# Scores of 8-wide heads in two row tiles of TensorE, and the additive mask as a 128-row matmul, in a two-layer decoder

## Time and profile before

| | |
|---|---|
| median of the runs | 787.25 us (786.77 to 790.87) |
| span of the profiled execution | 788.8 us; a time of its own beside the span is not listed |
| instructions | 12952 |
| TensorE matmul (PE) | 633.0 us busy, 80% |
| TensorE weight load (PEld) | 513.6 us, 65% |
| VectorE (DVE) | 505.0 us, 64% |
| ScalarE (ACT) | 381.3 us, 48% |
| GpSimd (POOL) | 230.7 us, 29% |
| mean granted clock of TensorE | 0.869 of 2.4 GHz |

### The profile page before, as it was taken

The page is one execution under the profiler, slowest core; times in us unless marked ns, Lnnn a source line. Parts: engine busy times, 40 slices in busy tenths (PEclk is TensorE's granted clock), DMA queues, the critical chain, the costliest instruction groups (busy, mean ns, idle before and its releaser), DMA issues. The chain is left out here.

```text
span 788.8 us, 12952 instructions
## 1 busy us (share of the span) xinstructions
PE 633.0 (80%) x3779; PEld 513.6 (65%) x3786; DVE 505.0 (64%) x1221; ACT 381.3 (48%) x966; POOL 230.7 (29%) x254
## 2 busy tenths in 40 slices
PE   4898885999999968699889999979999988781006
PEld 3777774777777756467668888868777776430006
DVE  3788983656675745744544444447677676469886
ACT  3778883445444532133235444435455463484615
POOL 3555552323222211356500000014334331005220
PEclk9899996989997958899979999989899797695558
DMA  5400000001000000000000000001010000000001
GB/s 158 160 11 10 10 13 14 21 21 28 24 20 17 0 1 1 0 1 2 1 11 7 11 10 7 17 14 27 20 26 21 19 17 0 1 0 0 0 0 54
DMA packets 30649, 15.29 MB, mean 19 GB/s; under 512 B 18513, under 2 KB 29841, under 8 KB 30610
## 3 DMA queue, kind: packets, MB, share of 16 engines
q1 hardware_dynamic: 30610, 14.82, 6.7%
HBM read 10.09 MB, written 1.05 MB: 14 GB/s over the span
## 5 line engine op out<-in xcount | busy, mean ns | idle before, releaser
L330 PE MATMUL bank<-a_mov,a_stat 128*128 128x256 f32 x256 | 84.2, 459 | 12.0 <-issue 10.2
L514 DVE TENSOR_REDUCE rowmax<-bank 128x8 f32<-128x512 f32 x64 | 44.2, 691 | 62.2 <-PE bank L330 61.4
L330 PEld LDWEIGHTS bank<-a_mov,a_stat 128*128 128x128 f32 x256 | 50.6, 219 | 28.7 <-issue 23.0
L1213 POOL TENSOR_TENSOR e_hid<-e_gated,e_relu 128x512 f32<-128x512 f32 x32 | 40.6, 1270 | 57.0 <-DVE e_gated L1328 56.8
L1088 PEld LDWEIGHTS bank<-body_sb,e_hid 128*128 128x128 f32 x288 | 37.7, 196 | 22.0 <-issue 13.9
L139 POOL TENSOR_TENSOR xb<-X,made_bias 128x128 f32<-128x128 f32 x32 | 14.6, 457 | 117.2 <-DVE r L149 103.8
L1190 ACT ACTIVATE e_relu<-bank 128x512 f32<-128x512 f32 x36 | 21.5, 598 | 54.2 <-PE bank L1066 45.1
L1328 DVE TENSOR_TENSOR e_gated<-e_relu,bank 128x512 f32<-128x512 f32 x32 | 21.9, 686 | 36.6 <-PE bank L1076 22.5
L252 POOL TENSOR_TENSOR a_stat<-qk,head_sb 128x512 f32<-128x512 f32 x32 | 33.3, 1041 | 37.5 <-ACT qk L405 36.3
L330 PE MATMUL bank<-l_mov,l_stat 128*128 128x256 f32 x128 | 42.3, 462 | 2.2 <-POOL l_mov L252 2.0
L469 ACT ACTIVATE oT<-bank 64x64 f32<-64x64 f32 x192 | 41.7, 217 | 4.1 <-PE bank L375 2.0
(11 more groups left out here) (262 smaller groups left out, 1716.3 us busy)
## 6 DMA issues: line engine op xcount, KB each, us to landing
kvT<-in_ctxT SPq DMA_DIRECT2D x64, 64.0 KB, 2.1
xs<-X SPq DMA_DIRECT2D x56, 64.0 KB, 1.9
body_sb<-in_body SPq DMA_DIRECT2D x2, 950.0 KB, 5.1
body_sb<-in_body SPq DMA_DIRECT2D x2, 949.5 KB, 5.2
out<-X SPq DMA_DIRECT2D x4, 256.0 KB, 2.3
X<-in_x SPq DMA_DIRECT2D x1, 896.0 KB, 6.0
mid_sb<-in_mid SPq DMA_DIRECT2D x1, 448.0 KB, 3.6
head_sb<-in_head SPq DMA_DIRECT2D x1, 422.0 KB, 3.2
```

What stands on the lines that cost most here:

```text
L330: mm = nc.tensor.matmul(psS[b][:, 256 * half:256 * half + 256], m.stat[:, par, b, 2 * half:2 * half + 2, :], m.mov[:, par, b, :, :], start ...
L514: nc.vector.tensor_reduce(m.rowmax[:, b, :], psS[b][:, :].rearrange("p (x k) -> p x k", k=T), AX.X, ALU.max).then_inc(s[f"max_done{b}"].se ...
L1213: nc.gpsimd.tensor_tensor(m.hid[:, n % DEEP, :], a, m.relu[:, n % DEEP, :], ALU.mult).then_inc(s["hid_ready"], 1)
```

## The change

The sixteen heads are dealt to two row tiles of the array: heads 0 to 7 are rows 0 to 63, heads 8 to 15 rows 64 to 127. With h = 8r + 4j + 2a + c the row tile is r. `stat` holds only two copies (for a or for c), `mov` four (for j and the other of the two). A product takes 64 rows, 128 stationary and 256 moving columns. There are four per tile, as before: for each sequence b first r = 0, then r = 1. The product of r goes to bank `psS[r]`, columns 256 b to 256 b + 255, so a bank holds half of the heads of both sequences, where it held all heads of one.

Both banks are written in one step, `scores`, which waits for both banks to be free. In the cross slot it stands where the scores of bank 0 stood; in the causal slot where the scores of bank 0 stood, in phase 0. The separate step for bank 1 is gone from both lists. All that reads a bank later (maximum, subtraction, exponential, turning, outputs, squares) takes half of the heads of both sequences with as many elements as before.

The mask has 128 rows, of which only row 0 is not zero, for ones and mask alike; both banks' mask products come ahead of the scores. For this a block at the start sets both operands to zero first: VectorE a memset of 128 x 1024 f32 columns, GpSimd one of the ones and a wait.

The diff, cut to its core (the readers of the banks change their access patterns likewise):

```diff
-        def mask_operand(t, par, out, which, mask, done):
+        def mask_operand(t, par, out, which, mask, n, done):
...
-                m.qk[:, par, which, :].rearrange("p (b k) -> p b k", b=SB).unsqueeze(2).broadcast_to([P, SB, 4, T]),
-                mask.unsqueeze(1).unsqueeze(3).broadcast_to([P, SB, 4, T]), ALU.mult).then_inc(s[done].sem, 1)
+                m.qk[:, par, which, :].rearrange("p (b k) -> p b k", b=SB).unsqueeze(2).broadcast_to([P, SB, n, T]),
+                mask.unsqueeze(1).unsqueeze(3).broadcast_to([P, SB, n, T]), ALU.mult).then_inc(s[done].sem, 1)
...
-            mask_operand(t, par, m.stat, 1 if causal else 0, m.mask_ca if causal else m.mask_ac, "stat_ready")
+            mask_operand(t, par, m.stat, 1 if causal else 0, m.mask_a if causal else m.mask_c, 2, "stat_ready")
...
-            mask_operand(t, par, m.mov, 0 if causal else 1, m.mask_i, "mov_ready")
+            mask_operand(t, par, m.mov, 0 if causal else 1, m.mask_jc if causal else m.mask_ja, 4, "mov_ready")
...
-        def scores(t, par, b):
+        def scores(t, par):
 
             wait_before(pe, before, "scores", t)
             wait(pe, s["stat_ready"], t + 1)
             wait(pe, s["mov_ready"], t + 1)
-            wait(pe, s[f"shifted{b}"], t)
+            wait(pe, s["shifted0"], t)
+            wait(pe, s["shifted1"], t)
+            rows = (slice(0, T), slice(T, P))
             if masked:
-                nc.tensor.matmul(psS[b][:, :], m.ones_bf[0:1, :],
-                                 w.mask_row[0:1, bass.ds(t * P + b * T, T)].unsqueeze(1).broadcast_to([1, 8, T]),
-                                 start=True, stop=False, skip_group_check=True)
-            for half in range(2):
-                mm = nc.tensor.matmul(psS[b][:, 256 * half:256 * half + 256], m.stat[:, par, b, 2 * half:2 * half + 2, :],
-                                      m.mov[:, par, b, :, :], start=not masked, stop=True, skip_group_check=masked)
-            mm.then_inc(s[f"s_psum{b}"].sem, 1)
+                for r in range(2):
+                    nc.tensor.matmul(psS[r][:, :], m.ones_bf[:, :],
+                                     w.mask_row[:, bass.ds(t * P, P)].rearrange("p (b k) -> p b k", b=SB)
+                                     .unsqueeze(2).broadcast_to([P, SB, 4, T]),
+                                     start=True, stop=False, skip_group_check=True)
+            for b in range(SB):
+                for r in range(2):
+                    mm = nc.tensor.matmul(psS[r][:, 256 * b:256 * b + 256], m.stat[rows[r], par, b, :, :],
+                                          m.mov[rows[r], par, b, :, :], start=not masked, stop=True, skip_group_check=masked)
+                    if b == SB - 1:
+                        mm.then_inc(s[f"s_psum{r}"].sem, 1)
...
             if causal:
-                run(turn, 0), run(scores1, 1), run(project_outputs, 3), run(project, 0), run(outputs0, 2)
-                run(outputs1, 2), run(values, 0), run(scores0, 0), run(turn_outputs, 2)
+                run(turn, 0), run(project_outputs, 3), run(project, 0), run(outputs0, 2)
+                run(outputs1, 2), run(values, 0), run(scores, 0), run(turn_outputs, 2)
             else:
-                run(turn, 0), run(scores0, 1), run(outputs1, 2), run(project, 0), run(scores1, 1), run(turn_probs0, 1)
+                run(turn, 0), run(scores, 1), run(outputs1, 2), run(project, 0), run(turn_probs0, 1)
                 run(values, 0), run(turn_outputs, 2), run(outputs0, 1), run(project_outputs, 2), run(turn_probs1, 1)
...
-    m.stat = sb("stat", [P, 2, SB, 4, T])
+    m.stat = sb("stat", [P, 2, SB, 2, T])
...
-        m.mask_row = sb("mask_row", [1, NSEQ * T], BF16)
-        m.ones_bf = sb("ones_bf", [1, P], BF16)
+        m.mask_row = sb("mask_row", [P, NSEQ * T], BF16)
+        m.ones_bf = sb("ones_bf", [P, P], BF16)
...
-                pool.memset(m.ones_bf[:, :], 1.0)
+                pool.memset(m.ones_bf[:, :], 0.0).then_inc(s["ones"], 1)
+                pool.wait_ge(s["ones"], 1)
+                pool.memset(m.ones_bf[0:1, :], 1.0)
...
+                nc.vector.memset(m.mask_row[:, :].bitcast(F32), 0.0)
                 nc.vector.memset(m.l_score[:, :, :], 0.0)
...
-                nc.vector.tensor_scalar(m.mask_row[:, :], m.mask_u8[:, :], 1.0, BIG, ALU.subtract, ALU.mult)
+                nc.vector.tensor_scalar(m.mask_row[0:1, :], m.mask_u8[:, :], 1.0, BIG, ALU.subtract, ALU.mult)
```

More of the change, by code:

```diff
@@ L235, in small_attention, with half_of_heads @@
     masked = not causal and w.mask_row is not None
+    def half_of_heads(prob, par, r):
+        return prob[:, par, :, 2 * r:2 * r + 2, :, :].rearrange("p b i c q -> p b (i c q)")
     def on_pool(pool):
@@ L266, in square1 @@
             wait(pool, s["o_psum1"], t - 1)
-            soft = m.soft[:, 1, :].rearrange("p (c i q) -> p c i q", c=2, i=NI)
-            nc.gpsimd.tensor_tensor(m.prob[:, par, 1, :, :, :].rearrange("p i c q -> p c i q"), soft, soft,
-                                    ALU.mult).then_inc(s["prob_ready1"].sem, 1)
+            soft = m.soft[:, 1, :].rearrange("p (b x) -> p b x", b=SB)
+            nc.gpsimd.tensor_tensor(half_of_heads(m.prob, par, 1), soft, soft, ALU.mult).then_inc(s["prob_ready1"].sem, 1)
         def add_bias(t, par):
@@ L329, in scores @@
-            for half in range(2):
-                mm = nc.tensor.matmul(psS[b][:, 256 * half:256 * half + 256], m.stat[:, par, b, 2 * half:2 * half + 2, :],
-                                      m.mov[:, par, b, :, :], start=not masked, stop=True, skip_group_check=masked)
-            mm.then_inc(s[f"s_psum{b}"].sem, 1)
[L334 to L340, removed]
-            wait_before(pe, before, "turn_probs", t)
[L342 to L346, removed]
+                for r in range(2):
[3 more added lines that the diff above has]
+                                     start=True, stop=False, skip_group_check=True)
@@ new lines, in scores, with turn_probs @@
+            for b in range(SB):
[4 more added lines that the diff above has]
+                        mm.then_inc(s[f"s_psum{r}"].sem, 1)
+        def turn_probs(t, par, r):
+            wait_before(pe, before, "turn_probs", t)
+            wait(pe, s[f"pT_ready{r}"], t)
+            wait(pe, s[f"exp_done{r}"], t + 1)
+            for b in range(SB):
+                for j in range(2):
+                    n = 2 * b + j
+                    mm = nc.tensor.transpose(psT[r][:, n * P:(n + 1) * P], m.prob[:, par, b, 2 * r + j, :, :], m.ident)
+            mm.then_inc(s[f"pT_psum{r}"].sem, 1)
@@ L352, in turn_probs1, with outputs @@
             turn_probs(t, par, 1)
-        def outputs(t, par, b):
+        def outputs(t, par, r):
             wait(pe, s["o_ready"], t)
             wait(pe, s["v_ready"], t + 1)
[L359 to L364, removed]
+            wait(pe, s[f"prob_ready{r}" if causal else f"pT_ready{r}"], t + 1)
+            for b in range(SB):
+                for j in range(2):
+                    i = 2 * r + j
+                    lhsT = m.prob[:, par, b, i, :, :] if causal else m.probT[:, r, 2 * b + j, :]
+                    at = 36 * (NI * b + i)
+                    mm = nc.tensor.matmul(psO[:, at:at + 36], lhsT, m.vals[:, par, b, i, :, :, :], start=True, stop=True)
+            mm.then_inc(s[f"o_psum{r}"].sem, 1)
         def outputs0(t, par):
@@ L420, in exponential @@
         def exponential(t, par, b):
-            sc = m.prob[:, par, b, :, :, :].rearrange("p i a k -> p (i a k)")
+            sc = half_of_heads(m.prob, par, b)
             if causal:
@@ L447, in square0 @@
             wait(act, s["o_psum0"], t - 1)
-            nc.scalar.activation(m.prob[:, par, 0, :, :, :].rearrange("p i c q -> p c i q"),
-                                 m.soft[:, 0, :].rearrange("p (c i q) -> p c i q", c=2, i=NI), ACT.Square).then_inc(s["prob_ready0"].sem, 1)
+            nc.scalar.activation(half_of_heads(m.prob, par, 0), m.soft[:, 0, :].rearrange("p (b x) -> p b x", b=SB),
+                                 ACT.Square).then_inc(s["prob_ready0"].sem, 1)
         def copy_probs(t, par, b):
@@ L520, in less_maximum @@
             wait(dve, s[f"pT_psum{b}"], t - 1)
[L521 to L524, removed]
+            nc.vector.tensor_tensor(m.prob[:, par, :, 2 * b:2 * b + 2, :, :].rearrange("p b j x k -> p b (j x) k"),
+                                    psS[b][:, :].rearrange("p (b i k) -> p b i k", b=SB, i=NI),
+                                    m.rowmax[:, b, :].rearrange("p (b i) -> p b i", b=SB).unsqueeze(3)
+                                    .broadcast_to([P, SB, NI, T]),
                                     ALU.subtract).then_inc(s[f"shifted{b}"].sem, 1)
@@ L1623, in _ @@
             apply(NC - 1)
-HEAD_COLS = [("ident", P), ("mask_ac", 4), ("mask_ca", 4), ("mask_i", NI), ("causal", T), ("w0_q", D), ("w0_k", D), ("w0_v", D), ("w0_o", D),
```

(17 more changed lines are left out.)

## The result

The changed kernel takes 830.0 us (median of five runs, 825.2 to 843.1), the one before 787.25 (786.4 to 790.9) beside it: ratio 1.0529, 95% interval 1.0464 to 1.0593. The changed kernel is slower, as forecast, but by 43 us and not by 9, and outside the range of 775 to 818.

The account below looks back on a forecast made before the run. Bound taken as a ring of TensorE and VectorE waits in the cross stages and ScalarE's own list in the causal one. Terms 6.5 + 0 - 2.4 + 0.6 + 4 = +8.7 gave 796 us on the median, range 775 to 818.

Parts of the forecast that it names:

- Clock: Three stages using the changed code: low clock in half as much time again, +4 us, ends -12 and +24.
- The other terms: Biased rotation +6.5, masked stage 0, causal clamp -2.4 and start +0.6 us.
- The rival of a doubled loss: Low clock loss in the three stages doubles as TensorE idles more: +29, 816 us; chance 0.12.
- Overlap: Scores block in two row tiles: eight passes take five pass times, ending 1.34 us after their start.
- The rival of no overlap: Eight score passes run in a row, rotation later by 1.15 us (biased) and 0.82 (masked): +32, 819 us; chance 0.12.
- Step between 64 and 128 rows: On TensorE, a row change costs the overlap of neighbours: the next matmul starts 0.02 us before the last one's end.
- Biased rotation, +6.5: Biased cross attention: rotation waits for later projections, 0.43 us a slot over 15 slots; ends 0 and +8.6.
- Masked stage, 0: Masked cross attention: rotation 0.10 us later, offset by bank 1's earlier exponential; 0 over 15 slots, ends -3 and +5.
- Causal clamp, -2.4: Causal stage: GpSimd's smaller operand lets VectorE's clamp end earlier, removing ScalarE's 0.16 us wait in 15 slots; ends 0 and -2.4.
- Start, +0.6: Kernel start: VectorE's added memset of 0.91 us delays TensorE, partly covered by SyncE's wait for weights; ends 0 and +0.91.
- B: Theory from the experiments, not the prediction: passes that use 64 rows hold the clock low, overlapped or not.
- C: Theory from the experiments, not the prediction: scores in one place of the slot instead of two lower the clock.

Follow-up runs that it names:

- e6: Changed kernel with row tiles kept, but bank 0 scored from tile 0 and bank 1 from tile 1 at the two old places: 950.95 us, ratio 1.1857.
- e5: Changed kernel with all four score products on row tile 0 (rows 0 to 63), so none can overlap: 942.74 us, ratio 1.1993.
- e2: Changed kernel with all 128 rows in every score product, same places, order, banks and mask: 829.53 us, ratio 1.0633.
- the fillers: Products of 128 rows that nobody reads, added to the changed kernel (771.33 us) and to the kernel before (765.69 us).
- e3: Changed kernel plus 128-row products that nobody reads, two per causal slot and two per cross slot: 771.33 us, ratio 0.9888.
- e4: Kernel before plus 128-row products that nobody reads, one per causal slot and two per cross slot: 765.69 us, ratio 0.9823.
- e1: Changed kernel with score products ordered by row tile, both sequences of tile 0 and then both of tile 1: 831.35 us, ratio 1.0718.
- e7: Kernel before with only the mask part of the change (128 rows with zeros, and the memsets at the start): 768.66 us, ratio 0.9794.
- e9: Kernel before plus products that nobody reads, one per causal slot and two per cross slot, of 64 rows: 779.74 us, ratio 0.9921.

## Why the prediction was wrong, by its own steps

**Clock: the step that failed.** It was forecast at +4, "a choice, with ends of -12 (half the loss goes) and +24 (it doubles)". The mechanism was named, low stretches at 1.2 GHz, but its size came from one idea, that the clock falls when TensorE has less to do, so that the loss scales with the work taken out. The runs put another cause in its place: scores on 64 rows in place of 128 keep the clock low, even where TensorE's record is full (e6) and nothing overlaps (e5), and the causal stage with 128 rows at the same place takes 125.73 in place of 148.59 (e2). Measured with the fillers, the term is about +37 (58.7 less 21.6), one and a half times its upper end. The other terms come to +4.7 in the forecast and to about 5.6 in e3 against e4; that these agree is partly luck, as two of them were off (below). The rival of a doubled loss named the right term, but tied it to idle time and stopped at 816. The prediction had the row that spoke against its idea, a slot before a fall with TensorE busy 7.90 of 8.52, and read from it only that no long idle stretch was needed.

The Trainium skill (TensorE: Matmul & The Clock Gate, Part 1) ties the gate to how busy TensorE has been and warns of idle gaps. That agrees with the fillers, and it does not cover e6, where the record is full and the clock low. Here the measurement decides: with passes of 64 rows a full record and a low clock go together.

**Overlap: better than forecast.** Five pass times were assumed from the order of issue; four were measured (1.14 against 1.34). The rival of no overlap is refuted. The Trainium skill (TensorE: Matmul & The Clock Gate, Part 3) says that matmuls on different row groups run side by side; the trace agrees, with 1.14 for eight passes.

**Step between 64 and 128 rows:** judged at 0.14 of lost overlap, measured 0.08 to 0.09 on either side of the scores (they start 0.07 before the turn's end, the outputs 0.08 before theirs; both were 0.16 before).

**Biased rotation, +6.5: the wait and its cost came, and the low clock hides them.** The changed kernel has no slot of this stage at the full clock in which all steps run; e1, with the same operations, has one, the fourth of the stage. Its slot and its rotation, and the fourth slot of the kernel before:

```profile
567.90:576.13 8.23, 6.75 (x49) 5.50 (x49) 5.98 (x16) 4.59 (x13) 2.75 (x4) 1.00 0.11 26
...
571.45 1.13 DVE L569 SCALAR_TENSOR_TENSOR l_rope<-bank,body_sb,mid_sb 128x128 f32<-128x128 f32 x4 [0.18 <-PE bank L309]
```

```profile
545.31:553.14 7.83, 7.08 (x49) 6.17 (x49) 6.20 (x16) 4.59 (x13) 3.18 (x4) 1.00 0.10 25
```

The rotation waits for the projections (L309) and starts 3.55 us after the turn against 3.15; bank 1's maximum follows 0.40 later too, and the slot takes 0.40 more, where 0.43 was forecast. Later slots can be compared only with fillers, and there less is left: 8.20 in e3 against 8.04 in e4, the means of the last eight.

**Masked stage, 0: held within its ends, as a sum of two misjudged parts.** At full clock the slots are nearly unchanged: the last four take 8.5 to 8.7, where the kernel before has 8.3 to 8.5. The mask's own gain was about 0.35 (e7), and the second mask ahead of the scores, 0.52 from the first mask to the scores against 0.22 in e7, gave it back. The pause before the mask, which the prediction took for a step between rows, did not go: the mask starts 0.31 after the turn and not 0.18.

**Causal clamp, -2.4: did not come.** The operand's write fell to 0.61 and the clamp to 0.64, and ScalarE's 0.16 for the clamp went, all as forecast. In its place ScalarE waits 0.19 us for VectorE at a later step, the square (e2, where this stage is at full clock):

```profile
77.40 0.61 POOL L256 TENSOR_TENSOR a_stat<-qk,head_sb 128x256 f32<-128x256 f32 x1 [1.52 <-ACT qk L412]
77.65 0.64 DVE L511 TENSOR_SCALAR a_soft<-a_score 128x512 f32<-128x512 f32 x1
...
80.80 0.63 ACT L455 ACTIVATE a_prob<-a_soft 128x512 f32<-128x512 f32 x1 [0.19 <-DVE a_soft L515]
```

6.65 a slot against 6.64. The prediction looked for what would be late next and named only the 0.80 for the projection; VectorE's product for the square was the closer one.

**Start, +0.6: right.** The stages begin 0.59 later (5.93 against 5.34), behind the new memset:

```profile
1.03 0.91 DVE L1778 MEMSET mask_row<- 128x1024 f32 x1 [1.03 <-PEq L1928]
...
5.93 0.45 PE L293 MATMUL bank<-head_sb,X 128*128 128x128 f32 x1 [5.93 <-PEq L1746]
```

**Open:** the split between B and C in the cross stages of the changed kernel (e6 shows B without C; e2 has a low clock with 128 rows, from the single place or from the longer block in it); the weight of a 64-row pass, and why the clock rises so seldom in e6; and why the stages between and after, whose code is the same, were 3.7 and 2.9 us shorter (their granted clock was 0.95 against 0.93 and 0.70 against 0.68).

## What to carry to other kernels

Where TensorE falls to its low clock for stretches, price a change first by what it does to the clock: halving the rows of the products can cost more than the passes it saves, and a slot at 2.4 GHz can look unchanged while the kernel slows. Compare slots at the same place of a stage: the first ones lack the steps of tiles that are not there yet. If TensorE has idle time off the critical path, try one or two products over all 128 rows that nobody reads, and measure. A one-row product among 128-row ones may be worth widening with zeros: here that alone took 2% off.

## What was not expected of the hardware

- The clock stays at 0.50 with TensorE's record full, 13.08 of 13.08 us and thirteen such slots in a row, if the scores use 64 rows (e6); with 128 rows the slot of this stage takes 7.82.
- Work without use makes the kernel faster: 830.0 to 771.3 (e3), 787 to 765.7 (e4).
- The order of the products is no matter for row tiles: with four passes of one tile in a row in the program (e1) or two (the changed kernel), eight take 1.14 us.
- The two one-row mask products cost some 0.35 us a slot more than such products of 128 rows, and low stretches besides: 14.9 us in the masked stage between the two traces (e7).
- Passes of 64 rows that are added in idle time lift the clock (0.869 before, 0.907 in e9, 0.908 with 128 rows in e4), while those that replace 128 rows let it stay low (e5, e6).
